# Layer norm, attention and an FP4 feed-forward on one core: another job table, row maxima split on VectorE, five score banks at the end

## The chip, the core and the metric

The kernel runs on one core of a Trainium2 chip. The metric is the device time in microseconds of one execution, the median of three runs. Times inside the kernel come from one execution recorded by the hardware profiler; there, PE is TensorE (PEld its weight loads), DVE VectorE, ACT ScalarE, POOL GpSimd and SP SyncE, whose queue issues all transfers.

## What is computed

Input x is 4 x 1024 x 128. Attention (16 heads of 8) and a gated feed-forward whose inputs and weights are rounded to FP4 in blocks of 16 run beside each other on the same normalized x, and both are added to x:

```python
def fp4_quant_dequant(x):
    scale = max(max(abs(block of 16)) / 6, 1e-12)
    return nearest of +-(0, .5, 1, 1.5, 2, 3, 4, 6) to block / scale, times scale

xn = layernorm(x)
scores = einsum('bhqd,bhkd->bhqk', q, k) * scale + alibi_bias
attn = softmax(scores) @ v @ Wo + bo
h = silu(fp4_linear(xn, w_gate)) * fp4_linear(xn, w_up)
out = x + attn + fp4_linear(h, w_down)
```

## The kernel before

**Units.** Attention runs in 256 units, numbered U: 4 batches x 4 quads of heads x 2 halves of the queries x 8 key tiles (KT = 8). In a unit TensorE makes four score products (one head's 128 keys by 512 queries each, `score`, L1067), ScalarE turns each into exponentials (`exponential`, L728), and one unit later TensorE multiplies the four by v (`value_product`, L1078, eight instructions) into one PSUM bank that fills over the eight key tiles of a half.

**Row maxima.** Softmax needs each query's maximum first. So 22 positions (LEAD) ahead of the scores TensorE makes the same products in the other layout, two chunks of 128 queries by 1024 keys per unit (`half_chunk`, L1048), and VectorE takes the negated maximum of each (`reduce_chunk`, L934). There are 512 chunks; the last are made in unit 244. After the 16 chunks of a half m (in unit 8m-4) the maxima are split into two bf16 parts, on GpSimd by `max_parts` at L630 and L631 (for half 0 on VectorE, L937 and L938), turned by TensorE (job "turn", unit 8m-3), copied by ScalarE and brought by SP through DRAM into two rows of the score operand (`max_rows`, L434 and L437). The first score of unit 8m waits for them.

**Jobs.** All else is cut into jobs, at most one in the middle of a unit and at most one at its end (turn and pvT). `plan()` gives each its unit: it is a table, and every engine walks the units and does its part of what the table says, in order. The feed-forward runs over 16 pairs of token tiles. Pair p has the jobs xT (transposes), gate 0 and 1, up 0 and 1, hT 0 and 1 (transposes of the rounded hidden values), down 0 and 1. Beside it stand xnT, q, k, v of later batches, ctxT and wo (context and output projection), and pvT, which turns a finished half of the value products; VectorE divides it (L949, L950).

**Rounding of a pair.** Behind gate 1 GpSimd does `swish` (L605, L606), behind each up `hidden` (L611). VectorE takes block maxima (`x_maxima`, `hidden_maxima`), then `block_scales` and `block_inverses`; GpSimd scales (`scale_to_grid`, L526, L528); VectorE masks the exponents (`powers`, L925); GpSimd adds and subtracts the power (`add_power` L537, L538; `take_power` L543) and scales back (`scale_back` L554, L562). hT (L1108) waits for that. Rounding job p+1 holds the hidden values of pair p and the x of pair p+1. Counted in units, VectorE's steps before stood at up 0 + 1 and + 2 and up 1 + 2 to + 4, GpSimd's at up 1 + 3, 5, 7, 8, and hT at up 1 + 10 or later (ROUNDED). GpSimd's loop takes a unit's jobs of U-1 first (swish, hidden, `add_down`, `add_wo`), then these steps.

**Banks.** Scores and the PSUM results of the jobs that ScalarE empties share a ring of three banks (`bank`, numbered by ST); the maxima's chunks and pvT share two slots of two banks (`slot`, numbered by MX). TensorE waits in `free_bank` for the use three back, in `free_slot` for the use two back. SP and GpSimd run through the same table; SP's `store` writes an output group of 512 tokens.

Of the kernel before, what the change touches and what calls it, by code (L numbers as in the profile page):

```python
# [13 lines left out]
P = 128  # L14
# [5 lines left out]
GT = 4  # L20
# [54 lines left out]
FFN_FIRST, FFN_LAST = 5, 237  # L75
# [24 lines left out]
ROUNDED = 10  # L100
# [10 lines left out]
def plan():  # L111
# [13 lines left out]
    for m in range(HALVES):  # L125
        if m >= LEAD // 16:
            put(turn_unit(m), "turn", m)
        put(KT * (m + 1) + 2, "pvT", m)
    x_at = put(FFN_FIRST, "xT", 0)
    for p in range(NP):  # L130
        U = put(x_at + 1, "gate", p, 0)
        U = put(U + 1, "gate", p, 1)
        U = put(U + 2, "up", p, 0)
        up = put(U + 1, "up", p, 1)
        U = put(up + ROUNDED, "hT", p, 0)
        U = put(U + 1, "hT", p, 1)
        if p + 1 < NP:
            x_at = put(FFN_FIRST + (FFN_LAST - FFN_FIRST) * (p + 1) // (NP - 1), "xT", p + 1)
        U = put(U + 1, "down", p, 0)
        put(U + 1, "down", p, 1)  # L140
    for b in range(1, B):
        for g in (2 * b, 2 * b + 1):
            U = norm_unit(b) + 1 + 8 * (g % 2)
# [3 lines left out]
            put(max(U, QUADS * UNITS * (b - 1) + 2) + 1, "v", g)  # L147
    for hb in range(2 * B):
        U = put(at["pvT", hb // 2 * 8 + 6 + hb % 2] + 1, "ctxT", hb)
        for i in range(2):  # L150
            U = put(max(U, at["down", 2 * hb + 1, 1]) + 1, "wo", hb, i)
# [54 lines left out]
def attn_ffn(nc, x, wq, bq, wk, bk, wv, bv, wo, bo, wg, wu, wd, out):  # L206
    with ExitStack() as ctx:
# [128 lines left out]

        def bank(*key):
            i = ST[key] % 3
            return low[:, 512 * i:512 * i + 512]

        def slot(*key):
            return mx[MX[key] % 2]
# [18 lines left out]
        def _(sp):  # L361
# [78 lines left out]
            def store(hb):  # L440
                g, i = hb, hb % 2
                sp.wait_ge(out_ok, 2 * hb + 2)
                sp.dma_start(out_tok[g * GT:(g + 1) * GT].rearrange("t p e -> p t e"),
                             o_s[i].rearrange("p (t e) -> p t e", e=E)).then_inc(stored[i], 16)
# [12 lines left out]
            for U in range(NU + 2 * KT):  # L457
# [10 lines left out]
                for job in JOBS.get(U - 3, ()):  # L468
                    if job[0] == "wo" and job[2] == 1:
                        store(job[1])  # L470
            for i in range(2):
                sp.wait_ge(stored[i], 16 + 16 * NG // 2)
# [3 lines left out]
        def _(pool):  # L476
# [149 lines left out]
            def max_parts(m):  # L626
                pool.wait_ge(mx_free, MX["max", 16 * m + 15] + 1)
                if m >= 2:
                    pool.wait_ge(st_full, ST["turn", m - 2] + 1)
                link(nc.gpsimd.tensor_copy(neg_parts[m % 2][:, 0:16], neg_max[m % 2][:]))  # L630
# [589 lines left out]
```

## Time and profile before

| | |
|---|---|
| median of 3 runs | 849.28 us (848.42 to 849.83) |
| the profiled execution | 847.38 us, span 845.5 us |
| TensorE busy | 772.5 us (91%) |
| VectorE busy | 693.8 us (82%) |
| ScalarE busy | 651.7 us (77%) |
| GpSimd busy | 416.8 us (49%) |
| DVE L934, 512 maxima | 613.8 us busy, 94.6 us idle before them, 86.1 of it for PE L1048 |
| ACT L728, 1024 exponentials | 559.0 us busy, 132.2 us idle before them, 126.4 of it for PE L1067 |

Busy shares are means over stages. What a change is worth is read from the distance between the starts of two value products, which is the length of a unit, and from what stands inside.

### The profile page before, as it was taken

Reading aid. Unit: us, or ns where it says so; the run is one execution under the profiler, and the core shown is the slowest. Engines: PE = TensorE matmul, PEld = TensorE weight load, DVE = VectorE, ACT = ScalarE, POOL = GpSimd, SP = SyncE. Lnnn points to the kernel's source line nnn. Section 1 sums busy time; section 2 is a strip of 40 time slices with the busy share of each in tenths; the row PEclk is TensorE's granted clock in tenths of the full one; section 3 lists DMA queues with packets and bytes.
Section 4 is the critical chain, followed back from the end, with each engine's and each line's share of the span. In section 5 each row is a group of like instructions: output and inputs, shape, how many; then the busy total and the mean of one; then the engine's idle time right before and its main releaser. Section 6 shows DMA issues by size and latency. Waiting matters only on the chain.

```text
span 845.5 us, 13893 instructions
## 1 busy us (share of the span) xinstructions
PE 772.5 (91%) x4939; PEld 231.1 (27%) x4939; DVE 693.8 (82%) x792; ACT 651.7 (77%) x1342; POOL 416.8 (49%) x413
## 2 busy tenths in 40 slices
PE   3289999999999999899999999999999999998986
PEld 2012223222232333222232333222222323232322
DVE  7797888988888888888888887889898898989710
ACT  4206888878878888788878888787878888788885
POOL 7365262571728373662548472662627262353242
PEclk9657999999999999999999999999999999999999
DMA  5820002041102020140101011230101000000000
GB/s 149 251 49 1 2 2 78 2 127 25 39 2 52 2 76 2 52 113 2 39 2 39 2 49 42 88 76 2 39 2 51 3 15 1 2 1 2 2 2 26
DMA packets 32828, 31.85 MB, mean 38 GB/s; under 512 B 4344, under 2 KB 26552, under 8 KB 32760
## 3 DMA queue, kind: packets, MB, share of 16 engines
q1 hardware_dynamic: 32760, 30.96, 13.6%
q8 instruction: 40, 0.66, 0.3%
q14 instruction: 28, 0.23, 0.1%
HBM read 15.91 MB, written 15.04 MB: 37 GB/s over the span
## 4 chain that ended last, share of the span: by engine, by line
PE 71%; DVE 18%; ACT 6%; issue 3%; DMA 1%; POOL 1%; SPq 0%; ACTq 0%; POOLq 0%; DVEq 0%
PE low L1078 25%; PE mx L1048 22%; DVE neg_max L934 13%; PE low L1067 6%; ACT probs L728 4%; PE low L1116 3%; PE low L1101 3%; PE low L1095 3%; PE low L1034 2%; PE mx L1127 2%; ACT pv_s L825 2%; PE low L1108 2%; PE low L1030 1%; DVE am L905 1%; PE low L1142 1%
## 5 line engine op out<-in xcount | busy, mean ns | idle before, releaser
L934 DVE TENSOR_REDUCE neg_max<-mx 128x1 f32<-128x1024 f32 x512 | 613.8, 1220 | 94.6 <-PE mx L1048 86.1
L728 ACT ACTIVATE probs<-low 128x512 f32<-128x512 f32 x1024 | 559.0, 609 | 132.2 <-PE low L1067 126.4
L1048 PE MATMUL mx<-k_op,q_op 51*128 51x512 bf16 x1024 | 316.5, 394 | 39.9 <-DVE neg_max L934 21.1
L1067 PE MATMUL low<-q_op,k_op 53*128 53x512 bf16 x1024 | 332.3, 385 | 12.3 <-ACT probs L728 8.5
L1078 PE MATMUL low<-probs,v_op 128*32 128x512 f32 x2048 | 273.6, 606 | 0.4
L1048 PEld LDWEIGHTS mx<-k_op,q_op 51*128 51x128 bf16 x1024 | 61.7, 94 | 313.8 <-issue 175.1
L1067 PEld LDWEIGHTS low<-q_op,k_op 53*128 53x128 bf16 x1024 | 74.4, 93 | 91.8 <-ACT probs L728 81.6
L630 POOL CAST neg_parts<-neg_max 128x16 bf16<-128x16 f32 x31 | 6.8, 220 | 155.1 <-DVE neg_max L934 82.9
L537 POOL TENSOR_SCALAR mb<-mb 128x960 f32<-128x960 f32 (+2 forms) x17 | 58.7, 3455 | 26.4 <-DVE mb L925 25.0
L1078 PEld LDWEIGHTS low<-probs,v_op 128*32 128x32 f32 x2048 | 40.3, 108 | 65.8 <-issue 32.2
L618 POOL TENSOR_TENSOR x_s<-x_s,down_s 128x128 f32<-128x128 f32 x32 | 14.6, 456 | 75.9 <-ACT down_s L761 54.3
L611 POOL TENSOR_TENSOR hid<-gate_s,up_s 128x352 f32<-128x352 f32 x32 | 30.0, 937 | 39.7 <-ACT up_s L755 37.5
L526 POOL TENSOR_TENSOR zb<-hid,inv 128x704 f32<-128x704 f32 x16 | 22.2, 1385 | 52.4 <-DVE inv L920 51.7
L605 POOL TENSOR_SCALAR tanh_s<-tanh_s 128x704 f32<-128x704 f32 x16 | 31.7, 1979 | 28.3 <-ACT gate_s L749 26.3
L543 POOL TENSOR_TENSOR zb<-zb,mb 128x960 f32<-128x960 f32 (+2 forms) x17 | 38.3, 2251 | 1.3 <-POOL neg_parts L631 0.5
L538 POOL TENSOR_TENSOR zb<-zb,mb 128x960 f32<-128x960 f32 (+2 forms) x17 | 38.2, 2245 | 1.4
L949 DVE RECIPROCAL pv_r<-mx 128x16 f32<-128x16 f32 x32 | 8.2, 255 | 34.6 <-PE mx L1127 34.1
L734 ACT COPY max_t<-low 32x128 bf16<-32x128 bf16 x32 | 8.1, 254 | 31.3 <-PE low L1056 31.0
L1116 PE MATMUL low<-dT_s,hqT 128*128 128x128 f32 (+1 forms) x192 | 29.6, 291 | 0.0
L606 POOL TENSOR_TENSOR gate_s<-tanh_s,gate_s 128x704 f32<-128x704 f32 x16 | 26.9, 1680 | 1.3
L1095 PE MATMUL low<-gT_s,xqT 128*128 128x352 f32 x64 | 27.5, 511 | 0.0
L1101 PE MATMUL low<-uT_s,xqT 128*128 128x352 f32 x64 | 27.5, 511 | 0.0
(128 smaller groups left out, 587.2 us busy)
## 6 DMA issues: line engine op xcount, KB each, us to landing
q_op<-q_rows SPq DMA_DIRECT2D x32, 192.0 KB, 3.8
k_op<-k_rows SPq DMA_DIRECT2D x32, 192.0 KB, 4.9
q_rows<-qp SPq DMA_DIRECT2D x8, 384.0 KB, 2.6
k_rows<-kp SPq DMA_DIRECT2D x8, 384.0 KB, 3.0
x_s<-in_L_attn_inputs_dram SPq DMA_DIRECT2D x8, 256.0 KB, 4.0
q_rows<-qp SPq DMA_DIRECT2D x8, 256.0 KB, 2.9
k_rows<-kp SPq DMA_DIRECT2D x8, 256.0 KB, 3.1
out_dram<-o_s SPq DMA_DIRECT2D x8, 256.0 KB, 2.4
```

The costliest lines, as they stand in the source:

```text
L537: link(nc.gpsimd.tensor_scalar(m, m, 1.0, ROUND, ALU.max, ALU.mult))
L538: link(nc.gpsimd.tensor_tensor(z, z, m, ALU.add))
L543: link(nc.gpsimd.tensor_tensor(z, z, m, ALU.subtract))
L605: link(nc.gpsimd.tensor_scalar(tanh_s[:], tanh_s[:], 1.0, None, ALU.add))
L728: nc.scalar.activation(probs[U % 3][:, 2 * g + x, :], bank("exp", U, j), ACT.Exp).then_inc(st_free, 1)
L934: nc.vector.tensor_reduce(to, slot("max", pos)[:], AX.X, ALU.max, negate=True).then_inc(mx_free, 1)
L1048: ins = nc.tensor.matmul(slot("max", pos)[:, 512 * kh:512 * kh + 512], q, k, start=True, stop=True)
L1067: nc.tensor.matmul(bank("exp", U, j), k_op[quad][r, g, kt * P:(kt + 1) * P], q_op[quad][r, g, half * HALF:(half + 1) * HALF], start=True, ...
L1078: ins = nc.tensor.matmul(pv[32 * hh:32 * hh + 32, :], v_op[b % 2][:, kt, 4 * quad + hh, :], probs[U % 3][:, hh, :], start=(kt == 0), stop= ...
L1095: nc.tensor.matmul(bank("gate", p, t)[:, 0:I], xqT[:, t * P:(t + 1) * P], gT_s[:], start=True, stop=True).then_inc(st_full, 1)
L1101: nc.tensor.matmul(bank("up", p, t)[:, 0:I], xqT[:, t * P:(t + 1) * P], uT_s[:], start=True, stop=True).then_inc(st_full, 1)
L1116: ins = nc.tensor.matmul(bank("down", p, t)[:, 0:P], hqT[t][0:n, c * P:(c + 1) * P], dT_s[0:n, c * P:(c + 1) * P], start=(c == 0), stop=(c ...
```

## The change

- `plan()`: a pair's jobs have least distances from its xT (`FROM_XT`): gates at 1 and 3, ups at 10 and 11, hT at 21 and 27, downs at 28 and 29, with hT at least 12 units behind up 1; pairs begin at units 6 to 229 instead of 5 to 237. The second norm group of a batch begins four units earlier, ctxT and wo and the last pvT are placed otherwise.
- VectorE's six steps of a rounding come one per unit, after the unit's second maximum; GpSimd's steps come two units later.
- The maxima of every half are split on VectorE, right after the last chunk's maximum; `max_parts` on GpSimd goes.
- From unit 245 the four scores alternate between the two halves of the array's rows. From unit 246 the ring of banks has five: the slot that isn't pvT's becomes two banks.
- The last group's wo isn't copied by ScalarE and added by GpSimd; VectorE adds it from PSUM, and the store is made in two halves.

The job table as it comes out: for pair 10, up at 164 and 165, gate of pair 11 at 170 and 172, hT at 177 and 181 (before: up at 167 and 168, gate of pair 11 at 176 and 177, hT at 178 and 179). Up 1 of the pairs 0 to 15 stands at 17, 31, 46, 61, 76, 91, 106, 121, 135, 150, 165, 180, 195, 210, 225, 240. The last units: hT 15 at 252 and 256, wo 6 at 253 and 255, down 15 at 257 and 258, the last pvT at the end of 257 (before: 258), ctxT 7 at 259, wo 7 at 260 and 262.

```diff
@@ -72,7 +72,7 @@
 HALVES = 2 * B * QUADS
-FFN_FIRST, FFN_LAST = 5, 237
+FFN_FIRST, FFN_LAST = 6, 229
@@ -97,7 +97,21 @@
-ROUNDED = 10
...
+LAST = (CHUNKS - LEAD) // 2
+RINGED = LAST + 1
+TAIL_BANKS = 5
...
+def head(U, j):
+    return HEAD[j] if U < LAST else HEAD[2 * (j % 2) + j // 2]
...
+FROM_XT = {("gate", 0): 1, ("gate", 1): 3, ("up", 0): 10, ("up", 1): 11, ("hT", 0): 21, ("hT", 1): 27,
+           ("down", 0): 28, ("down", 1): 29}
+ROUNDED = 12
@@ -125,30 +139,27 @@
             put(turn_unit(m), "turn", m)
-        put(KT * (m + 1) + 2, "pvT", m)
-    x_at = put(FFN_FIRST, "xT", 0)
+        put(KT * (m + 1) + (2 if m + 1 < HALVES else 1), "pvT", m)
     for p in range(NP):
-        U = put(x_at + 1, "gate", p, 0)
-        U = put(U + 1, "gate", p, 1)
-        U = put(U + 2, "up", p, 0)
-        up = put(U + 1, "up", p, 1)
-        U = put(up + ROUNDED, "hT", p, 0)
-        U = put(U + 1, "hT", p, 1)
-        if p + 1 < NP:
-            x_at = put(FFN_FIRST + (FFN_LAST - FFN_FIRST) * (p + 1) // (NP - 1), "xT", p + 1)
-        U = put(U + 1, "down", p, 0)
-        put(U + 1, "down", p, 1)
+        start = FFN_FIRST + (FFN_LAST - FFN_FIRST) * p // (NP - 1)
+        U = put(start, "xT", p)
+        for kind in ("gate", "up", "hT", "down"):
+            if kind == "hT":
+                U += ROUNDED - 1
+            for t in range(2):
+                U = put(max(U + 1, start + FROM_XT[kind, t]), kind, p, t)
...
         for g in (2 * b, 2 * b + 1):
-            U = norm_unit(b) + 1 + 8 * (g % 2)
+            U = norm_unit(b) + 1 + 4 * (g % 2)
...
             put(max(U, QUADS * UNITS * (b - 1) + 2) + 1, "v", g)
+    U = 0
     for hb in range(2 * B):
-        U = put(at["pvT", hb // 2 * 8 + 6 + hb % 2] + 1, "ctxT", hb)
+        U = put(max(U, at["pvT", hb // 2 * 8 + 6 + hb % 2], at["down", 2 * hb + 1, 1] - 1) + 1, "ctxT", hb)
         for i in range(2):
-            U = put(max(U, at["down", 2 * hb + 1, 1]) + 1, "wo", hb, i)
+            U = put(max(U, at["down", 2 * hb + 1, 1]) + 1 + i, "wo", hb, i)
@@ -334,12 +345,18 @@
+        tail = ST["exp", RINGED, 0]
+        pvT_slot = MX["pvT", HALVES - 2] % 2
...
         def bank(*key):
-            i = ST[key] % 3
+            n = ST[key]
+            if n >= tail and (n - tail) % TAIL_BANKS < 2:
+                return mx[1 - pvT_slot][:, 512 * ((n - tail) % TAIL_BANKS):][:, 0:512]
+            i = (n if n < tail else tail + (n - tail) % TAIL_BANKS - 2) % 3
...
         def slot(*key):
-            return mx[MX[key] % 2]
+            return mx[pvT_slot if key == ("pvT", HALVES - 1) else MX[key] % 2]
@@ -437,11 +454,11 @@
-            def store(hb):
-                g, i = hb, hb % 2
-                sp.wait_ge(out_ok, 2 * hb + 2)
-                sp.dma_start(out_tok[g * GT:(g + 1) * GT].rearrange("t p e -> p t e"),
-                             o_s[i].rearrange("p (t e) -> p t e", e=E)).then_inc(stored[i], 16)
+            def store(g, t0, t1):
+                i = g % 2
+                sp.wait_ge(out_ok, 2 * g + t1 * 2 // GT)
+                sp.dma_start(out_tok[g * GT + t0:g * GT + t1].rearrange("t p e -> p t e"),
+                             o_s[i][:, t0 * P:t1 * P].rearrange("p (t e) -> p t e", e=E)).then_inc(stored[i], 16)
@@ -467,9 +484,12 @@
                     if job[0] == "wo" and job[2] == 1:
-                        store(job[1])
+                        if job[1] + 1 < NG:
+                            store(job[1], 0, GT)
+            for t in (0, GT // 2):
+                store(NG - 1, t, t + GT // 2)
             for i in range(2):
-                sp.wait_ge(stored[i], 16 + 16 * NG // 2)
+                sp.wait_ge(stored[i], 16 + 16 * NG // 2 + 16 * i)
@@ -623,15 +643,6 @@
-            def max_parts(m):
-                pool.wait_ge(mx_free, MX["max", 16 * m + 15] + 1)
-                if m >= 2:
-                    pool.wait_ge(st_full, ST["turn", m - 2] + 1)
-                link(nc.gpsimd.tensor_copy(neg_parts[m % 2][:, 0:16], neg_max[m % 2][:]))
-                link(nc.gpsimd.tensor_tensor(neg_parts[m % 2][:, 16:32], neg_max[m % 2][:], neg_parts[m % 2][:, 0:16],
-                                             ALU.subtract))
-                pool.sem_inc(parts_max_ok, 1)
@@ -640,9 +651,6 @@
                 b, u = divmod(U, QUADS * UNITS)
-                for m in range(1, HALVES):
-                    if U == turn_unit(m) - 1:
-                        max_parts(m)
@@ -652,17 +660,17 @@
                         add_down(job[1], job[2])
-                    elif job[0] == "wo":
+                    elif job[0] == "wo" and job[1] + 1 < NG:
...
                     up = AT["up", p, 1]
-                    if U == up + 3:
+                    if U == up + 5:
                         scale_to_grid(p + 1)
-                    if U == up + 5:
+                    if U == up + 7:
                         add_power(p + 1)
-                    if U == up + 7:
+                    if U == up + 9:
                         take_power(p + 1)
-                    if U == up + 8:
+                    if U == up + 10:
@@ -723,7 +731,7 @@
                 if U < NU:
-                    x, g = HEAD[j]
+                    x, g = head(U, j)
@@ -759,7 +767,7 @@
                     nc.scalar.copy(down_s[:, t * P:(t + 1) * P], bank("down", p, t)[:, 0:P]).then_inc(st_free, 1)
-                elif kind == "wo":
+                elif kind == "wo" and p + 1 < NG:
@@ -932,8 +940,10 @@
                 nc.vector.tensor_reduce(to, slot("max", pos)[:], AX.X, ALU.max, negate=True).then_inc(mx_free, 1)
-                if pos == 15:
+                if pos % 16 == 15:
                     dve.wait_ge(mx_free, MX["max", pos] + 1)
+                    if m >= 2:
+                        dve.wait_ge(st_full, ST["turn", m - 2] + 1)
@@ -979,26 +989,37 @@
+            def add_last_wo(hb, i):
+                to = o_s[hb % 2][:, i * PW:(i + 1) * PW]
+                dve.wait_ge(st_full, ST["wo", hb, i] + 1)
+                dve.wait_ge(down_ok, 2 * NP)
+                dve.wait_ge(stored[hb % 2], (hb // 2 + 1) * 16)
+                nc.vector.tensor_tensor(to, bank("wo", hb, i)[:, 0:PW], x_s[:, hb * GW + i * PW:hb * GW + (i + 1) * PW],
+                                        ALU.add).then_inc(out_ok, 1)
...
                     for job in middle(U) if i == 1 else ():
-                        job_on_vector(job)
+                        if job[0] in IN_DVE_RING:
+                            job_on_vector(job)
+                        elif job[0:2] == ("wo", NG - 1):
+                            add_last_wo(job[1], job[2])
...
                             x_maxima(p + 1)
-                        if (U, i) == (up0 + 2, 0):
+                        if (U, i) == (up0 + 2, 1):
                             hidden_maxima(p + 1, 0)
-                        if (U, i) == (up1 + 2, 0):
+                        if (U, i) == (up1 + 2, 1):
                             hidden_maxima(p + 1, 1)
-                        if (U, i) == (up1 + 2, 1):
+                        if (U, i) == (up1 + 3, 1):
                             block_scales(p + 1)
-                        if (U, i) == (up1 + 3, 0):
+                        if (U, i) == (up1 + 4, 1):
                             block_inverses(p + 1)
-                        if (U, i) == (up1 + 4, 1):
+                        if (U, i) == (up1 + 6, 1):
@@ -1007,11 +1028,17 @@
             def free_bank(*key):
-                if ST[key] >= 3:
+                if ST[key] >= tail:
+                    if ST[key] < tail + 2:
+                        pe.wait_ge(mx_free, MX["max", CHUNKS - 1] + 1)
+                    pe.wait_ge(st_free, ST[key] - TAIL_BANKS + 1)
+                elif ST[key] >= 3:
...
             def free_slot(*key):
-                if MX[key] >= 2:
+                if key == ("pvT", HALVES - 1):
+                    pe.wait_ge(mx_free, MX["pvT", HALVES - 2] + 1)
+                elif MX[key] >= 2:
@@ -1058,7 +1085,7 @@
                 b, quad, half, kt = unit_of(U)
-                x, g = HEAD[j]
+                x, g = head(U, j)
```

## Rows read from the trace of the kernel before

**Rows 1.** The page, part 4: engines' shares of the chain that ended last.

```profile
PE 71%; DVE 18%; ACT 6%; issue 3%; DMA 1%; POOL 1%; SPq 0%; ACTq 0%; POOLq 0%; DVEq 0%
```

**Rows 2.** Timeline, value products of TensorE: start us, us, engine, line, operation, tiles.

```profile
74.87 1.07 PE L1078 MATMUL low<-probs,v_op 128*32 128x512 f32 x8
...
121.04 1.07 PE L1078 MATMUL low<-probs,v_op 128*32 128x512 f32 x8
...
123.50 1.06 PE L1078 MATMUL low<-probs,v_op 128*32 128x512 f32 x8
...
126.55 1.06 PE L1078 MATMUL low<-probs,v_op 128*32 128x512 f32 x8
...
129.50 1.06 PE L1078 MATMUL low<-probs,v_op 128*32 128x512 f32 x8
...
350.90 1.06 PE L1078 MATMUL low<-probs,v_op 128*32 128x512 f32 x8
...
354.37 1.07 PE L1078 MATMUL low<-probs,v_op 128*32 128x512 f32 x8
...
806.17 1.06 PE L1078 MATMUL low<-probs,v_op 128*32 128x512 f32 x8
```

**Rows 3.** Timeline of units 239 and 240; in brackets idle time before and releaser.

```profile
786.11 2.55 DVE L934 TENSOR_REDUCE neg_max<-mx 128x1 f32<-128x1024 f32 x2 [0.40 <-PE mx L1048]
...
788.41 0.09 PEld L1048 LDWEIGHTS mx<-k_op,q_op 51*128 51x128 bf16 x1 [0.84 <-issue]
...
788.95 0.55 PE L1108 MATMUL low<-ident,hq 128*128 128x128 f32 x3
...
790.04 0.09 PEld L1067 LDWEIGHTS low<-q_op,k_op 53*128 53x128 bf16 x1 [0.39 <-ACT probs L728]
```

**Rows 4.** Timeline, powers on VectorE and GpSimd's chain behind them.

```profile
455.30 0.73 POOL L624 TENSOR_TENSOR o_s<-o_s,x_s 128x256 f32<-128x256 f32 x1
...
548.03 0.66 DVE L925 TENSOR_SCALAR mb<-zb 128x960 int32<-128x960 int32 x1 [0.53 <-POOLq L531]
...
548.78 3.42 POOL L537 TENSOR_SCALAR mb<-mb 128x960 f32<-128x960 f32 x1 [0.83 <-DVE mb L925]
...
558.25 0.62 POOL L562 TENSOR_TENSOR xq<-zb,sc 128x256 f32<-128x256 f32 x1
...
559.06 1.98 POOL L605 TENSOR_SCALAR tanh_s<-tanh_s 128x704 f32<-128x704 f32 x1 [0.20 <-ACT probs L728]
...
561.12 1.68 POOL L606 TENSOR_TENSOR gate_s<-tanh_s,gate_s 128x704 f32<-128x704 f32 x1
```

**Rows 5.** Timeline, VectorE and GpSimd at work at the same time.

```profile
58.69 0.17 DVE L937 CAST neg_parts<-neg_max 128x16 bf16<-128x16 f32 x1
...
58.89 3.67 POOL L543 TENSOR_TENSOR zb<-zb,mb 128x1632 f32<-128x1632 f32 x1
...
58.90 0.17 DVE L938 TENSOR_TENSOR neg_parts<-neg_max,neg_parts 128x16 bf16<-128x16 f32 x1
...
168.51 1.16 POOL L594 TENSOR_TENSOR kr<-kf,kp 128x512 f32<-128x512 f32 x1
...
168.80 1.38 DVE L925 TENSOR_SCALAR mb<-zb 128x960 int32<-128x960 int32 x1
```

**Rows 6.** Timeline, scores and exponentials of unit 248.

```profile
812.10 0.24 PEld L1067 LDWEIGHTS low<-q_op,k_op 53*128 53x128 bf16 x3 [0.84 <-DMA q_op<-m_rows]
...
812.58 2.06 ACT L728 ACTIVATE probs<-low 128x512 f32<-128x512 f32 x4 [0.39 <-PE low L1067]
```

**Rows 7.** Timeline, the last steps.

```profile
834.88 1.07 PE L1078 MATMUL low<-probs,v_op 128*32 128x512 f32 x8
...
837.32 0.60 PE L1127 MATMUL mx<-ident,pv_s 128*128 128x128 f32 x4
...
840.08 1.13 PE L1142 MATMUL low<-wo_s,ctxT_s 128*128 128x128 f32 x8 [0.77 <-ACT ctxT_s L787]
...
841.25 1.40 POOL L624 TENSOR_TENSOR o_s<-o_s,x_s 128x256 f32<-128x256 f32 x2 [2.91 <-ACT o_s L766]
```

## The prediction

> **What bounds the kernel now.** I read the page's chain first [rows 1]: TensorE stands on 71% of it, VectorE on 18%. That averages over units of different kinds, so next come the starts of the value product, one per unit [rows 2]. The lengths fall on few values. An empty unit takes 2.46 us (121.04 to 123.50), a unit with any job 2.95 (126.55 to 129.50), whichever job it is; a pvT at a unit's end adds 0.59 (123.50 to 126.55 is 3.05). So a job costs a turn of the three-bank ring, 0.49 us, wherever it stands, and moving jobs alone wins nothing: from unit 3 to 245 both schedules hold 183 units with a job and 30 pvT. What varies is the rest. I compared all 244 starts (first 74.87, last 806.17) with the length of a like unit; some thirty units are too long by over 0.05 us, 10.5 us in all. Nearly all are empty units, or the unit after them, in which VectorE has feed-forward work beside two maxima, and one place is a late `max_parts` on GpSimd (350.90 to 354.37 is 3.47 for an empty unit). In a unit with a job VectorE has room: before its two maxima it idles 0.40 us [rows 3].
>
> **Part 1, VectorE's work on units with jobs: 9.3 us less.** x maxima, two hidden maxima, scales, inverses and powers now fall at up+1 to up+6. With the pair's period of about 15 units these are the units of the previous pair's hT1 and downs and of the next pair's xT and gate, so all but the powers sit beside jobs. Of the 10.5 us I leave 1.2: pair 0 and 1 (units 18, 19, 32), and unit 52, where powers and the split meet in an empty unit. An estimate, bounds 6 and 10.5.
>
> **Part 2, GpSimd's chain behind the powers: 10.6 us more by itself.** hT waits for the scale-back of its pair. From the masking multiply (548.78) to the scale-back's end (558.87) GpSimd needs 10.1 us, and the next engine step sees it 0.2 later [rows 4]. The old schedule allowed the same five units for it, from up+5 to up+10, and in no pair did the next pair's swish lie in them. Now powers come at up+6, `add_power` at up+7, hT at up+12, and the next pair's second gate job lies at up+7, so GpSimd's swish is queued between `add_power` and `take_power`: 559.06 to 562.80, 3.8 us [rows 4]. The chain is 14.1 us. It can start 0.8 us after the start of unit up+7 if the unit before has a job, 1.25 if it is empty (the second maximum ends later there): maxima end about 0.2 us after the next unit starts [rows 3], then 0.65 of powers and 0.1 to GpSimd [rows 4]. The array reaches hT 0.54 us after its unit's start (788.41 to 788.95) [rows 3]. Pair 10: units 172 to 176 are one with a job and four empty, 2.95 + 4 x 2.46 = 12.8, so hT is reached at 13.3 and ready at 15.35: 2.0 us late. Done for each pair from the job table, with 0.73 for an `add_wo` queued in between (455.30 is one) in pairs 4, 5, 9, 11 and 12: pairs 1, 2, 4, 5, 6, 9, 10, 11, 12, 13 are late by 0.85, 2.0, 0.8, 1.25, 0.95, 1.5, 2.0, 1.3, 0.75, 0.95: 12.3 us. Pairs 0, 3, 7, 8 (jobs fill the five units), 14 (no x part) and 15 are in time. TensorE waits in order, so behind hT stand the unit's second maxima products, two scores and the value product, and everything that needs them. Of each, 0.17 is slack: the array waits for ScalarE's second exponential a little later anyway (790.04) [rows 3]. 12.3 - 1.7 = 10.6.
>
> **Part 3, the split on VectorE.** It removes two GpSimd instructions per half and adds two to VectorE, 0.17 us each and 0.34 together with the gap [rows 5]. Beside a job that is covered by the 0.40 of idle time and the bank's slack; seven of 31 stand in empty units, where a lone short instruction costs nothing now either. The price is elsewhere: both read SBUF while GpSimd may be working. A powers instruction took 1.38 instead of 0.66 us [rows 4, 5]; it began at 168.80 while GpSimd's subtraction ran from 168.51 to 169.67, and ended half a microsecond after that: it was held until the running instruction ended. For the split's cast I take the same. For its subtraction, with two SBUF operands, the trace has one case, 58.90, 0.17 long and begun with a GpSimd add of 3.67 us (58.89): not held, but begun at the same moment. So the bounds are nothing and one whole GpSimd instruction, 0.6 to 3.4 us. I take the upper: an instruction that arrives in the middle of GpSimd's is nearer to the powers row, and the cast ends after GpSimd's next instruction of the chain is due, which follows its forerunner by 0.08 us (561.04 to 561.12 [rows 4]).
>
> The Trainium skill, "SBUF — State Buffer", section "Who interferes with whom", says that GpSimd's port pair is VectorE's second pair and an exclusive lock held for a whole instruction, which casts and tensor_scalar can take, and that a VectorE instruction with two SBUF inputs contends with a GpSimd one that reads SBUF. The powers row agrees with the first; by the second the subtraction is held and my upper value stands, by the 58.90 row alone it isn't.
>
> Splits come at units 8m-4. Those of m = 9, 11, 13, 15, 22, 24, 26 and 28 fall into GpSimd's chain of pairs 3, 4, 5, 6, 10, 11, 12, 13. Example m = 22, pair 10, times from unit 172's start: the cast is due at 3.0, held by the masking multiply to 4.6; the subtraction held by the add to 6.9; the next maximum runs 7.1 to 8.3 instead of 3.6 to 4.8; the products of unit 174, due at 5.4, need its slot: 2.9 us late. That takes the place of the 2.0 us at hT, it isn't added to it. So worked, the losses of pairs 1 to 6 and 9 to 13 are 0.85, 2.0, 1.9, 1.05, 1.6, 2.4, 1.5, 2.9, 1.45, 0.75, 1.9: 18.3 us, less 0.7 of slack for the four of hT alone, 17.6.
>
> **Part 4, the last units: 3.8 us less.** From unit 246 there are no maxima and four exponentials take 2.06 us, with 0.39 idle until the array's scores [rows 6]: three banks don't carry ScalarE over a value product. Five do. Ten units at 0.39, and 0.1 more in the four with a job: 4.3. Against it, scores of unit 248 waited last for the maxima's rows by DMA [rows 6] at 812.10, with two units of 2.45 behind the turn; two of 2.06 leave up to 0.8 uncovered, I take 0.5. The other order of heads (alternate row halves) shortens only TensorE, which isn't last there. Bounds 2.5 and 4.6.
>
> **Part 5, the final chain: 1.7 us less.** From the last value product (834.88) the pvT comes at 837.32 behind both downs [rows 7]; ahead of the second down it comes about 0.6 earlier. The last output went through a ScalarE copy and a GpSimd add that ended 842.65, 2.57 after the wo products began at 840.08; one VectorE add per half, an estimated 0.4 us (a maximum over 1024 columns takes half of 2.55 [rows 3]), ends some 1.5 after them. With a half-size last store I say 1.7 in all, bounds 1 and 2.2. Stores, the second-gate gap, the norm jobs four units earlier (q, k, v still come before their parts are due), and `xT` of pair 0 a unit later cost nothing: their consumers are units away.
>
> **Sum.** -9.3 - 3.8 - 1.7 + 17.6 = +2.8 us. The profiled execution took 847.38 (span 845.5), 1.9 under the median of the three runs, which I take as scatter: 849.28 + 2.8 = 852.1.
>
> **Rivals.** A, the forecast: late hT and held splits. B, only the cast, or neither, is held: the 58.90 row speaks for it. Then -14.8 + 10.6 = -4.2: 845.1, faster. It decides at 14.8 us of stalls; above it the change loses. C, GpSimd's chain isn't late and splits aren't held: the old chain had its two to three us of room in some pairs; against it, 3.8 us of swish is in the program's order. -14.8, with 1 for q and k parts in the way of the splits: 835.5. D, the change doesn't do what it says: VectorE's 10.5 us more of splitting (31 x 0.34) bring back most of the overflow, 7 us on top of A: 859. Against it is the idle time of units with a job.
>
> **Chances.** A 0.50, B 0.27, C 0.11, D 0.12. A's own range is 847 to 857, from its bounds. The range 840 to 858 takes in A and B and part of D, and leaves out C and the rest. A change under 0.2%, 1.7 us, can't be told from none. From A 0.35 slower, 0.08 same, 0.07 faster; from B 0.02, 0.03, 0.22; C faster, D slower: slower 0.49, same 0.11, faster 0.40.
>
> **What will show it.** Starts of value products: overflow in empty units gone (part 1). A wait of TensorE's hT loads for GpSimd's scale-back, 1 to 2 us in ten pairs; if absent, part 2 is wrong. VectorE's split subtraction with a duration up to 2 us, and maxima products waiting for maxima behind it; if all are 0.17, B. ScalarE without gaps after unit 246. The split in the final stretch: end of last value product to end of span 8.9 us instead of 10.6.

## The result

The changed kernel takes 841.8 us (median of 4, 840.1 to 842.9) against 849.6 us (848.4 to 853.5) of the kernel before: ratio 0.991, 95% interval 0.988 to 0.994. It is 7.8 us faster. A second set on another occasion gave 841.5 against 849.5 us, ratio 0.991 (0.989 to 0.993). The forecast was 852.1 us, slower; the measured time lies inside its range, on the other side of no change.

Spans of the profiled executions: 845.5 us before, 838.3 after. The page after, with the chain and the group of the maxima (busy, mean ns of one, idle before and what ended most of it):

```profile
span 838.3 us, 13876 instructions
...
PE 70%; DVE 8%; ACT 8%; POOL 8%; issue 3%; DMA 1%; SPq 1%; ACTq 0%; POOLq 0%; DVEq 0%
...
L942 DVE TENSOR_REDUCE neg_max<-mx 128x1 f32<-128x1024 f32 x512 | 612.5, 1221 | 79.8 <-PE mx L1075 70.2
```

Against [rows 1], VectorE has gone from 18% of the chain to 8%, and GpSimd, which had 1%, has 8%. That is a mean over all stages. Where the time went is read from the starts of the value products, one per unit, as in [rows 2]. The 244th to the 247th of them after:

```profile
803.21 1.06 PE L1105 MATMUL low<-probs,v_op 128*32 128x512 f32 x8
...
805.66 1.06 PE L1105 MATMUL low<-probs,v_op 128*32 128x512 f32 x8
...
807.23 1.06 PE L1105 MATMUL low<-probs,v_op 128*32 128x512 f32 x8
...
809.29 1.06 PE L1105 MATMUL low<-probs,v_op 128*32 128x512 f32 x8
```

The 244th starts at 803.21, and at 803.23 before: no time is won by then. Behind it units take 2.45, 1.57 and 2.06 us, and the last value product starts at 829.62 instead of 834.88 [rows 7]. I measure three stretches in every trace: the **body**, from the first value product to the 244th, the **tail**, from there to the last, and the **end**, from the last to the end of the span.

| | body | tail | end |
|---|---|---|---|
| before | 732.3 | 31.65 | 10.6 |
| after | 731.9 | 26.4 | 8.7 |

The body, to which the job table, VectorE's six units and the split belong, has won 0.4 us, as good as nothing. All of the gain is the other two: 5.2 us of tail and 1.9 of end. A like unit is one with the same kind of job at the same place of a half; by how much a unit is longer, I call its excess. In the body of the trace after, the excess is 10.0 us in all, against 10.5 before, but in other units: those of hT, and the unit behind the two longest. In the names of units I count as the job table does, so hT of pair 10 stands in unit 177.

### The profile page after: what moved, and what is told of

It is laid out like the page before. It is cut to its first block, busy times and chain, and to the rows that moved or that the text cites. A ratio compares the mean times of both kernels' runs of the same rounds, so it can differ in the third digit from the quotient of the medians.

```text
span 838.3 us, 13876 instructions
## 1 busy us (share of the span) xinstructions
PE 772.6 (92%) x4939; PEld 231.2 (28%) x4939; DVE 709.8 (85%) x856; ACT 649.7 (77%) x1340; POOL 401.9 (48%) x349
## 4 chain that ended last, share of the span: by engine, by line
PE 70%; DVE 8%; ACT 8%; POOL 8%; issue 3%; DMA 1%; SPq 1%; ACTq 0%; POOLq 0%; DVEq 0%
PE low L1105 25%; PE mx L1075 22%; DVE neg_max L942 6%; PE low L1094 6%; ACT probs L736 6%; PE low L1143 3%; PE low L1128 3%; PE low L1122 2%; PE low L1061 2%; PE mx L1154 2%; ACT pv_s L833 2%; POOL zb L563 2%; PE low L1135 2%; POOL zb L558 1%; POOL mb L557 1%
## 5 line engine op out<-in xcount | busy, mean ns | idle before, releaser
L736 ACT ACTIVATE probs<-low 128x512 f32<-128x512 f32 x1007 | 549.0, 608 | 123.8 <-PE low L1094 118.3
L1094 PE MATMUL low<-q_op,k_op 53*128 53x512 bf16 x1007 | 326.4, 387 | 13.4 <-ACT probs L736 7.9
L625 POOL TENSOR_SCALAR tanh_s<-tanh_s 128x704 f32<-128x704 f32 x16 | 31.7, 1983 | 26.1 <-ACT gate_s L757 25.0
L742 ACT COPY max_t<-low 32x128 bf16<-32x128 bf16 x32 | 8.2, 255 | 31.6 <-PE low L1083 31.2
L1143 PE MATMUL low<-dT_s,hqT 128*128 128x128 f32 x180 | 28.0, 292 | 0.0
L626 POOL TENSOR_TENSOR gate_s<-tanh_s,gate_s 128x704 f32<-128x704 f32 x16 | 26.9, 1683 | 1.3
L1143 PEld LDWEIGHTS low<-dT_s,hqT 128*128 128x128 f32 x180 | 22.3, 190 | 12.7 <-issue 11.0
```

The lines of the kernel that those rows point to most:

```text
L625: link(nc.gpsimd.tensor_scalar(tanh_s[:], tanh_s[:], 1.0, None, ALU.add))
L736: nc.scalar.activation(probs[U % 3][:, 2 * g + x, :], bank("exp", U, j), ACT.Exp).then_inc(st_free, 1)
L1094: nc.tensor.matmul(bank("exp", U, j), k_op[quad][r, g, kt * P:(kt + 1) * P], q_op[quad][r, g, half * HALF:(half + 1) * HALF], start=True, ...
L1143: ins = nc.tensor.matmul(bank("down", p, t)[:, 0:P], hqT[t][0:n, c * P:(c + 1) * P], dT_s[0:n, c * P:(c + 1) * P], start=(c == 0), stop=(c ...
```

## Experiment 1: the end alone, the split alone

**tail_alone.** The kernel before with `head`, the ring of five, the last pvT, `add_last_wo` and the halved store; `plan()`, all steps and `max_parts` as before. Its core, the rest left out:

```diff
+            n = ST[key]
+            if n >= tail and (n - tail) % TAIL_BANKS < 2:
+                return mx[1 - pvT_slot][:, 512 * ((n - tail) % TAIL_BANKS):][:, 0:512]
```

> The kernel before with only the two end parts of the change: alternate heads and five banks from the end of the maxima on, last pvT a unit earlier, the last output added by VectorE and stored in two halves. The two traces give 5.2 us for units 246 to 255 and 1.9 for what follows. Theory T (the whole gain is the end; job table, six units and split cancel): 849.5 - 7.1 = 842.4 us, the same as the changed kernel. Rival (the body's part of the change wins something the alignment of traces hides): above 844 us.

Measured: 843.0 us, ratio 0.993 (0.991 to 0.995), 6.8 us under the kernel before of the same call. Body 731.8, tail 26.9. The end parts are worth nearly all of the change, and the body's three parts together about nothing: 1 us by the times of two calls, nothing by the bodies (731.8 and 731.9).

**tail_and_split.** tail_alone with the split of every half on VectorE and no call of `max_parts`. The line that decides:

```diff
-                if pos == 15:
+                if pos % 16 == 15:
```

> tail_alone (old job table and steps, new end) with the split of every half on VectorE. By the trace of before the late split at unit 94 cost 1.6 us and the rest of VectorE's overflow 8.9; the split adds 0.34 us to VectorE in 31 units and is held by GpSimd in some. Theory: 843.0 - 1.6 + 0 to 3: 841.5 to 844.5 us, so the split alone is worth nothing that can be told. Rival (the split was the change's gain in the body): below 840 us.

Measured: 842.9 us, ratio 0.995 (0.993 to 0.996). The body grew from 731.8 to 734.6 us. Units 94 and 95 still exceed their like by 0.97 and 0.38 us, but for another reason. In tail_alone VectorE idles 0.69 us there for GpSimd's hidden product, which stands behind `max_parts`. In tail_and_split that wait is gone, and VectorE spends the same time on its own split, 0.17 us of cast and 0.52 of a subtraction that is held. And units 110, 158 and 174, which hold a split beside other steps of VectorE in empty units, grew by 0.4 to 0.8. The split alone gains nothing.

## Experiment 2: swish in GpSimd's chain

The trace after, GpSimd around pair 10 (columns as in [rows 4]):

```profile
589.36 3.42 POOL L557 TENSOR_SCALAR mb<-mb 128x960 f32<-128x960 f32 x1 [5.14 <-DVE mb L933]
592.87 2.22 POOL L558 TENSOR_TENSOR zb<-zb,mb 128x960 f32<-128x960 f32 x1
595.18 1.98 POOL L625 TENSOR_SCALAR tanh_s<-tanh_s 128x704 f32<-128x704 f32 x1
597.24 1.69 POOL L626 TENSOR_TENSOR gate_s<-tanh_s,gate_s 128x704 f32<-128x704 f32 x1
599.01 2.23 POOL L563 TENSOR_TENSOR zb<-zb,mb 128x960 f32<-128x960 f32 x1
601.32 1.39 POOL L574 TENSOR_TENSOR hq<-zb,sc 128x704 f32<-128x704 f32 x1
602.66 0.62 POOL L582 TENSOR_TENSOR xq<-zb,sc 128x256 f32<-128x256 f32 x1
```

And what waited, TensorE's transposes of hT in the same trace, pairs 10 and 2:

```profile
239.06 0.55 PE L1135 MATMUL low<-ident,hq 128*128 128x128 f32 x3 [2.16 <-POOLq L585]
...
603.48 0.52 PE L1135 MATMUL low<-ident,hq 128*128 128x128 f32 x3 [1.89 <-POOLq L585]
```

Swish (L625, L626) does lie between the power's add and its subtraction, the chain is 13.9 us where [rows 4] gives 10.1, and TensorE stands still for it. **swish_later** moves only that:

```diff
-                for job in JOBS.get(U - 1, ()):
+                for job in JOBS.get(U - 5, ()):
                     if job[0] == "gate" and job[2] == 1:
                         swish(job[1])
-                    elif job[0] == "up":
+                for job in JOBS.get(U - 1, ()):
+                    if job[0] == "up":
```

> The changed kernel with one thing moved: GpSimd does swish four units later than before (behind the scale-back of the pair before, still ahead of its own hidden products). Theory S (swish between add_power and take_power makes hT late): the array's waits at hT go, 3.8 us earlier ready; the unit lengths over the norm at units 43, 58, 59, 103, 118, 162, 177, 178, 222 go, 8.6 us in all, 2.3 of it the halved clock behind the two long waits; 833 us. Rival H (hT is late for another reason, VectorE's held casts and powers): waits stay, 841 us. Rival C (the clock falls by itself): waits go but units 59 and 178 stay long, 835.5 us.

Measured: 835.7 us, ratio 0.984 (0.982 to 0.986). Its body is 726.2 us, 5.7 less than the changed kernel's. All waits at hT for GpSimd are gone, and so are the long units 59 and 178: theory S, not H, and not C. A part of the gain is H's all the same: in the changed kernel units 118 and 222 (pairs 6 and 13, 0.6 us too long each) had TensorE wait 0.51 and 0.53 us for maxima behind a held cast, and only 0.23 for GpSimd. With GpSimd's work shifted these two casts take 0.29 and 0.30 instead of 1.11 and 1.12. That it is 835.7 and not 833 has a place too: units 86 and 102, quiet in the changed kernel, became 1.0 and 1.1 us too long. With swish gone from between, another GpSimd instruction meets the split there. The timeline of swish_later at the first:

```profile
321.45 2.23 POOL L563 TENSOR_TENSOR zb<-zb,mb 128x960 f32<-128x960 f32 x1
321.71 2.00 DVE L948 CAST neg_parts<-neg_max 128x16 bf16<-128x16 f32 x1
...
323.75 0.17 DVE L949 TENSOR_TENSOR neg_parts<-neg_max,neg_parts 128x16 bf16<-128x16 f32 x1
323.76 0.76 POOL L644 TENSOR_TENSOR o_s<-o_s,x_s 128x256 f32<-128x256 f32 x1
...
325.11 0.39 PE L1076 MATMUL mx<-k_op,q_op 51*128 51x512 bf16 x1 [0.72 <-DVE neg_max L943]
```

A cast of sixteen elements takes 2.00 us. It began in GpSimd's subtraction (321.45 to 323.68) and ended 0.03 us after it. The maxima queue behind it, and then TensorE waits 0.72 us for a slot.

## Experiment 3: is the subtraction held?

The changed kernel's own splits showed a part of what the forecast had counted on. Its trace, at the splits of halves 28 and 26:

```profile
688.41 0.17 DVE L947 CAST neg_parts<-neg_max 128x16 bf16<-128x16 f32 x1
688.46 0.72 POOL L644 TENSOR_TENSOR o_s<-o_s,x_s 128x256 f32<-128x256 f32 x1
688.62 0.60 DVE L948 TENSOR_TENSOR neg_parts<-neg_max,neg_parts 128x16 bf16<-128x16 f32 x1
...
733.71 2.23 POOL L563 TENSOR_TENSOR zb<-zb,mb 128x960 f32<-128x960 f32 x1
...
734.85 1.12 DVE L947 CAST neg_parts<-neg_max 128x16 bf16<-128x16 f32 x1
...
736.00 0.18 DVE L948 TENSOR_TENSOR neg_parts<-neg_max,neg_parts 128x16 bf16<-128x16 f32 x1
736.02 1.41 POOL L574 TENSOR_TENSOR hq<-zb,sc 128x704 f32<-128x704 f32 x1
```

Eight casts of 32 took 0.39 to 1.12 us, seven of them to 0.03 us after the end of a GpSimd instruction; the eighth, 0.55 us at 324.73, was let go while a GpSimd TENSOR_SCALAR ran on. But only one subtraction of 32 was held, that at 688.62, where GpSimd had got in during the cast. Count from the end of the instruction that holds the cast, 735.94 for the last one: the cast ends 0.03 us later, the subtraction starts 0.03 after that (736.00), and GpSimd's next instruction 0.08 after its forerunner's end (736.02). VectorE is first by 0.02 us.

Nor does every GpSimd instruction hold a cast. The forecast's own example was pair 10, where the split meets the masking multiply (589.36 to 592.78, shown above):

```profile
591.57 0.18 DVE L947 CAST neg_parts<-neg_max 128x16 bf16<-128x16 f32 x1
591.78 0.18 DVE L948 TENSOR_TENSOR neg_parts<-neg_max,neg_parts 128x16 bf16<-128x16 f32 x1
```

Both ran their usual time in the middle of it, though the like multiply of 271.58 held a cast from 274.09 to its end, 0.94 us. In all traces of this case a GpSimd TENSOR_TENSOR held every cast and subtraction of a split that met it with more than 0.3 us left to run; a GpSimd TENSOR_SCALAR held some and not others. What decides there stays open.

**cast_twice** spoils the order behind a held cast:

```diff
                     link(nc.vector.tensor_copy(neg_parts[m % 2][:, 0:16], neg_max[m % 2][:]))
+                    link(nc.vector.tensor_copy(neg_parts[m % 2][:, 0:16], neg_max[m % 2][:]))
```

> The changed kernel with the split's cast done twice, so that the subtraction comes 0.2 us later after a held cast. Theory G (the subtraction is held like the cast by a GpSimd instruction that runs, and in the changed kernel only slipped into GpSimd's 0.08 us gap, 0.03 us behind the cast): subtractions behind a held cast are now 0.6 to 2.3 us long in six to nine of 31 splits, and the kernel loses 2 to 6 us, 844 to 848 us. Rival N (two SBUF operands are never held except by the rare add_wo): all stay 0.17, and 31 casts of 0.2 us are covered: 842 us.

Measured: 856.0 us, ratio 1.009 (1.006 to 1.011): 14 us more than the changed kernel, for 32 instructions of 0.2 us. Its trace at the first such place of the body:

```profile
277.72 0.93 DVE L947 CAST neg_parts<-neg_max 128x16 bf16<-128x16 f32 x1
...
278.69 0.17 DVE L948 CAST neg_parts<-neg_max 128x16 bf16<-128x16 f32 x1
278.71 2.24 POOL L558 TENSOR_TENSOR zb<-zb,mb 128x960 f32<-128x960 f32 x1
278.90 2.09 DVE L949 TENSOR_TENSOR neg_parts<-neg_max,neg_parts 128x16 bf16<-128x16 f32 x1
...
282.18 0.39 PE L1076 MATMUL mx<-k_op,q_op 51*128 51x512 bf16 x1 [0.83 <-DVE neg_max L942]
```

The second cast takes the gap, GpSimd's add starts, the subtraction is held 2.09 us to its end. Nine subtractions are so lengthened, one of 3.47 us before the first value product; the body is 742.3 us, 10.4 over the changed kernel's. Theory G holds, and its price was set too low (2 to 6 us). The forecast's mechanism exists; the changed kernel escapes it by 0.02 us. The escape needs the 0.08 us between two GpSimd instructions. Where GpSimd's next one follows without a gap, as the second of the scale-back does, the subtraction is held behind a held cast too, from swish_later's unit 102:

```profile
372.26 0.62 POOL L582 TENSOR_TENSOR xq<-zb,sc 128x256 f32<-128x256 f32 x1
372.37 0.54 DVE L949 TENSOR_TENSOR neg_parts<-neg_max,neg_parts 128x16 bf16<-128x16 f32 x1
```

The Trainium skill says both ("SBUF — State Buffer", section "Who interferes with whom": a two-input VectorE instruction contends with a GpSimd one that reads SBUF, and issue order decides who blocks). The 2.09 us agree with the first and the two orders above with the second; the subtraction at 591.78, 0.18 us beside a GpSimd multiply that reads SBUF, does not agree with the first.

**split_by_maxima** takes the two held kinds away from swish_later. A maximum over one element is the cast, the same with its sign turned gives the negative, and a sum over two elements subtracts (`neg_max` is made 32 columns wide for it):

```diff
-                    link(nc.vector.tensor_copy(neg_parts[m % 2][:, 0:16], neg_max[m % 2][:]))
-                    nc.vector.tensor_tensor(neg_parts[m % 2][:, 16:32], neg_max[m % 2][:], neg_parts[m % 2][:, 0:16],
-                                            ALU.subtract).then_inc(parts_max_ok, 1)
+                    nm, hi = neg_max[m % 2], neg_parts[m % 2]
+                    link(nc.vector.tensor_reduce(hi[:, 0:16], nm[:, 0:16].unsqueeze(2), AX.X, ALU.max))
+                    link(nc.vector.tensor_reduce(nm[:, 16:32], hi[:, 0:16].unsqueeze(2), AX.X, ALU.max, negate=True))
+                    with nc.allow_low_precision(reason="two terms"):
+                        nc.vector.tensor_reduce(hi[:, 16:32], nm[:].rearrange("p (a c) -> p c a", a=2), AX.X,
+                                                ALU.add).then_inc(parts_max_ok, 1)
```

> swish_later with the split made of three small TENSOR_REDUCE instructions instead of a cast and a subtraction (the cast is a maximum over one element, the negative of it another, the low part a sum over two). Theory G (casts and two-operand subtractions are held by a GpSimd instruction that runs, TENSOR_REDUCE isn't, as the hidden maxima that overlap GpSimd's work show with 0.51 us): every split instruction takes 0.17 us, the 3.49 and 3.59 us of the empty units 86 and 102 fall to 2.5, 0.2 us more per split is covered, 835.7 - 2 to 3 = 833 us. Rival N (what delays those units is the place of the split, not the hold): they stay long, 836 us or more.

Measured: 833.4 us, ratio 0.984 (0.982 to 0.987), in another call than swish_later. At the place that took 2.00 us its trace has:

```profile
320.85 2.23 POOL L563 TENSOR_TENSOR zb<-zb,mb 128x960 f32<-128x960 f32 x1
...
321.10 0.17 DVE L949 TENSOR_REDUCE neg_parts<-neg_max 128x16 bf16<-128x16 f32 x1
321.31 0.17 DVE L950 TENSOR_REDUCE neg_max<-neg_parts 128x16 f32<-128x16 bf16 x1
321.51 0.19 DVE L952 TENSOR_REDUCE neg_parts<-neg_max 128x16 bf16<-128x32 f32 x1
```

Three instructions beside GpSimd's, none held, and units 86 and 102 are of the common length. The place of the split was not the fault, its kind was. The two kernels and the changed one were then timed once more beside each other:

> swish_later again, beside the next one on the same chip: 834 to 836.5 us.

> split_by_maxima again, beside swish_later_2. Its body, first value product to that of unit 245, was 1.3 us shorter in the traces (724.9 against 726.2 us). Theory G: 1 to 3 us under swish_later_2. Rival: no difference beyond 0.5 us.

> The changed kernel beside the two before it on the same chip. Theory S: 5.5 to 7 us over swish_later_2.

Measured: 836.4, 835.0 and 841.5 us, ratios 0.985, 0.984 and 0.991, each with some 0.002 to either side. swish_later's gain over the changed kernel is confirmed at 5.2 us. split_by_maxima is 1.4 us ahead of it, with intervals that overlap; the bodies of two traces each (727.1 and 726.2 against 724.1 and 724.9) say 2.1 us. Both beat the kernel before and the changed one; the last step is shown by the traces, not by the times.

## Experiment 4: the split on GpSimd

**split_on_gpsimd** is the changed kernel with `max_parts` of halves 1 to 31 back in GpSimd's loop, ahead of a unit's jobs; **swish_later_split_on_gpsimd** the same of swish_later. The call that comes back:

```diff
+                for m in range(1, HALVES):
+                    if U == turn_unit(m) - 1:
+                        max_parts(m)
```

> The changed kernel with the split of halves 1 to 31 back on GpSimd, as before the change. Theory S: GpSimd's chain also waits for a half's last maximum in eight pairs, hT waits grow by 1 to 3 us in each where the split stands behind add_power, 848 to 855 us. Rival V (the split's place costs and gives nothing, VectorE's casts held up to 1.1 us weigh as much): 840 to 843 us.

> swish_later with the split of halves 1 to 31 back on GpSimd. Theory Q (the split's two 0.2 us instructions cost GpSimd its wait for a half's last maximum, which stands behind add_power in eight pairs; with swish out of the chain it has 3.8 us of room for that): hT waits return in two to four pairs, 836 to 841 us. Rival R (the split's place matters only with swish in the chain): 833.5 to 836 us, since VectorE's held casts go too.

Measured: 852.4 us, ratio 1.004 (1.002 to 1.006), and 836.0 us, ratio 0.986 (0.984 to 0.988). In the trace of the first, pair 10:

```profile
599.73 0.20 POOL L650 CAST neg_parts<-neg_max 128x16 bf16<-128x16 f32 x1 [7.38 <-DVE neg_max L954]
...
600.43 3.42 POOL L557 TENSOR_SCALAR mb<-mb 128x960 f32<-128x960 f32 x1 [0.20 <-POOL neg_parts L651]
...
614.51 0.88 PE L1145 MATMUL low<-ident,hq 128*128 128x128 f32 x3 [4.78 <-POOLq L585]
```

GpSimd idled 7.38 us, and the half's last maximum ended it. Not all of that is the split's: the powers were done at 597.40 (596.75 and 0.65), so the wait for the maximum costs the chain 2.33 us, and the two instructions with their gaps 0.70. The masking multiply is queued behind them, and TensorE waits 4.78 us for hT where it waited 1.89. There are eleven such waits at hT, 18.9 us in all, against six and 6.7 us in the changed kernel. So in the new table the split on VectorE is worth 10.6 us with swish in the chain (of two calls; the ratios are 1.004 and 0.991). Without swish there it is worth nothing that can be told: 836.0 against 835.7 and 836.4 us, and the body is 725.4 against 726.2 and 727.1.

Of the forecasts for the second run, Q is right on what happens and R on what it costs: five waits at hT are back, in pairs 5, 6, 10, 12 and 13, but of 0.41 to 0.96 us each, and only unit 103 is longer by over 0.15 us for one (0.6). The run also tells what the rest of the body's change is worth. From tail_alone it differs by the job table, the units of the steps and the place of swish, and its body is 6.4 us shorter (725.4 against 731.8).

## Experiment 5: what of the tail did it

**three_banks** and **old_head_order**, both from swish_later:

```diff
-            if n >= tail and (n - tail) % TAIL_BANKS < 2:
-                return mx[1 - pvT_slot][:, 512 * ((n - tail) % TAIL_BANKS):][:, 0:512]
-            i = (n if n < tail else tail + (n - tail) % TAIL_BANKS - 2) % 3
+            i = n % 3
...
```

```diff
-    return HEAD[j] if U < LAST else HEAD[2 * (j % 2) + j // 2]
+    return HEAD[j]
```

> swish_later with three banks to the end; the other order of heads and the final chain stay. Theory B (the ring bounds the last units): units 246 to 255 return to about 2.45 us, ScalarE idles 0.4 us in each, 4.5 to 5.5 us more than swish_later of the same call. Rival P (the order of heads carries it): under 2 us more.

> swish_later with the old order of heads in the last units (two scores of one half of the array's rows behind each other); five banks stay. Theory B (ScalarE bounds these units, TensorE has time to spare): units of 2.06 stay, 835.7 to 836.2 us. Rival P (the pairing of row halves carries the end's gain): units 246 to 255 grow by 0.2 us each, 838 us.

Measured: 841.8 us, 5.4 over swish_later_2 of its call, tail 31.2 instead of 26.3 us; and 836.5 us, tail 27.3. In three_banks the units are back at 2.45, from its trace:

```profile
805.47 1.06 PE L1100 MATMUL low<-probs,v_op 128*32 128x512 f32 x8
807.92 1.06 PE L1100 MATMUL low<-probs,v_op 128*32 128x512 f32 x8
810.37 1.07 PE L1100 MATMUL low<-probs,v_op 128*32 128x512 f32 x8
```

The ring is worth 4.8 us of tail. The order of heads is worth 0.8 to 1.0 us by the traces (27.3 against 26.5 and 26.3 in two traces of swish_later) and nothing that can be told by the times; I had put it at nothing. Units 246 to 250 are the same, but the units with a job take 2.54 and 2.71 instead of 2.12 and 2.28, so there the array's time does count.

## Why the prediction was wrong

**The step that failed** is in part 3, the held subtraction. With it the losses at hT and behind splits were to be 17.6 us, 7.0 more than by hT alone; they measured 8.6. The bounds were right, and both ends exist on the chip (0.17 us, and 2.09 in cast_twice). The choice between them was wrong. It rests on the sentence that the cast ends after GpSimd's next instruction is due, 0.08 us behind its forerunner. A held cast doesn't take its 0.17 us anew once it is let go: it ends 0.03 us after the instruction that held it, and the subtraction starts at 0.06, before the 0.08. So one subtraction of 32 was held, for 0.60 us, instead of the forecast's eight. [rows 5] had the other half: there GpSimd starts at 58.89, the subtraction at 58.90, and it takes 0.17, so to start level was enough. Without this term the sum is -4.2, rival B, 845.1 us, the right sign.

The held cast was right in kind (eight cases, up to 1.12 us), but not in the forecast's own example: in pair 10, where 2.9 us were to be lost behind it, the cast took 0.18 us in the middle of the multiply. Where casts were held, six of the eight cost next to nothing; those of pairs 6 and 13 made TensorE wait 0.5 us, and it then waited less at hT.

That 841.8 us lies inside the range is no merit of the forecast, which took in rival B. From B's -4.2 to what was measured it is another 3.4 us: 2.0 at hT (part 2), 1.4 in the tail (part 4), and 0.2 each way in the other two.

**Part 1** held. Of 10.5 us of units too long, about 1.4 are left after, besides those of hT: 9.1 less, 9.3 forecast. That is counted in the traces; the run that has these parts without swish in the chain shows 6.4 us net (Experiment 4). One reading under it was rough: not every job makes 2.95 us. A q or k job makes 3.13, a v job 3.16, and any job in the first unit of a half 3.44. It cost nothing, as both tables have nearly as many of these (23 and 24 of the last kind).

**Part 2** held in mechanism, and was 2.0 us too large. Of the ten pairs, six came as worked out: by how late hT starts against its place in a unit in time, pairs 1, 2, 6, 9, 10 and 13 were late by 0.9, 2.2, 0.9, 1.45, 2.0 and 0.9 us for 0.85, 2.0, 0.95, 1.5, 2.0 and 0.95. Pairs 4, 5, 11 and 12, with an `add_wo` in the chain, had 0.2, 0.6, 0.6 and 0 for 0.8, 1.25, 1.3, 0.75. In 4 and 11 the five units were 0.8 and 0.6 us longer than the job table's sum; in 5 and 12 the multiply began 1.3 and 1.2 us after a value product's start, where the forecast's 0.8 after the unit's start makes 1.8. So hT was late by 9.8 us in all, for 12.3. The units of hT are 6.3 us too long, not 10.6: most of them took up 0.3 to 0.4 us, for which I had 0.17. But 2.3 us came behind them, which I hadn't counted. They bring it to 8.6, and swish_later takes all of it away.

**Part 4** was 1.4 us too small: 3.8 forecast, 5.2 measured. Exponentials run without gaps as told, and the maxima's DMA was waited for (0.45 us at unit 248). What I had at nothing was the order of heads (0.8), and unit 246, which takes 1.57 us; that scores run ahead there into the free banks is my reading, no run shows it by itself.

**Part 5**: 1.7 forecast, 1.9 measured. The trace after shows the chain as described, VectorE's two adds last, 0.87 us for both:

```profile
829.62 1.07 PE L1105 MATMUL low<-probs,v_op 128*32 128x512 f32 x8 [0.37 <-ACT probs L736]
...
831.49 0.63 PE L1154 MATMUL mx<-ident,pv_s 128*128 128x128 f32 x4
...
834.27 1.13 PE L1169 MATMUL low<-wo_s,ctxT_s 128*128 128x128 f32 x8 [0.77 <-ACT ctxT_s L795]
834.99 0.87 DVE L997 TENSOR_TENSOR o_s<-low,x_s 128x256 f32<-128x256 f32 x2 [2.26 <-PE low L1169]
```

Against [rows 7], pvT comes 1.87 us after the last value product instead of 2.44, the last addition ends 6.24 after it instead of 7.77. By these terms the change is -9.1 + 8.6 - 5.2 - 1.9 = -7.6 us; the spans say -7.2, and the 0.4 between them is the start: the first value product comes at 71.28 after and at 70.90 before. That start is scatter: in the two traces of swish_later it is 71.33 and 70.51, in those of split_by_maxima 70.56 and 73.86.

## What to carry to other kernels

When steps of an engine that works in order are spread to take load off another, list the queue of each engine between producer and consumer and look for a long step of the next iteration that now stands in between: 3.8 us of swish ate the gain of the body, and moving one line gave back 5.2 us. Keep instructions of the kinds that two engines exclude each other with out of VectorE's critical queue, however short they are; a cast of 16 elements took 2.00 us, a reduction that does the same 0.17. When asking who gets in first behind an instruction that both wait for, count both engines from its end: here 0.06 us against 0.08, and one more instruction in between turned it.

## What the hardware showed that I had not expected

A stall on TensorE can cost more than its length. Granted clock (PEclk, 1.00 is 2.4 GHz) of the trace after around pair 2's hT, where the array stood from about 236.9 to 239.06:

```profile
core 0: us, PE busy (x) PEld busy (x) DVE busy (x) ACT busy (x) POOL busy (x), PEclk, DMA share, GB/s
230.00:236.00 6.00, 5.92 (x42) 1.11 (x40) 5.80 (x6) 5.21 (x11) 5.75 (x4) 1.00 0.00 1
236.00:239.00 3.00, 0.90 (x8) 0.12 (x4) 1.90 (x2) 1.81 (x4) 2.79 (x3) 1.00 0.00 0
239.00:240.30 1.30, 1.24 (x7) 0.44 (x7) 0.00 (x0) 0.59 (x2) 0.00 (x0) 0.66 0.00 0
240.40:242.40 2.00, 2.00 (x11) 0.23 (x9) 1.22 (x1) 0.88 (x2) 0.00 (x0) 0.50 0.00 0
242.40:245.00 2.60, 2.37 (x20) 1.33 (x16) 1.70 (x3) 1.34 (x3) 0.00 (x0) 0.92 0.00 0
```

After 2.16 us of waiting the clock fell to 0.50, 1.2 GHz, and by 243.2 it was back: a maxima product takes 0.39 us there, and 0.60 at 239.54. The value product in between took 1.94 us instead of 1.07, and unit 59 was 1.07 us too long without any wait of its own; the same followed pair 10's wait of 1.89 us (unit 178, 1.18 too long), and not pair 9's of 1.37. In swish_later there is neither the waits nor the long units.

The length of the wait alone doesn't decide it. The same kernel, run once more as changed_again, has the same wait at pair 10 and keeps its clock. The array's row, and the window behind it (columns as above):

```profile
604.27 0.52 PE L1135 MATMUL low<-ident,hq 128*128 128x128 f32 x3 [1.88 <-POOLq L585]
...
604.30:606.30 2.00, 2.00 (x17) 0.57 (x19) 0.94 (x1) 1.47 (x3) 0.00 (x0) 1.00 0.03 8
```

Its unit 178 is not too long. And in cast_twice two waits of 0.80 and 0.83 us, with one matmul of 0.22 between them (428.56), were followed by 0.50 (431.70 to 433.70), and the unit behind was 1.09 us too long. So a part of what cast_twice costs is the clock's.
